# Normalized rows laid over the turned ones, other engine orders in the route stage, repacks by ScalarE, stores of stacked rows awaited one stage later

## The reference, cut to what matters

```python
xn = _layernorm(x)                       # 8 x 512 rows of 256
# attention branch, 16 heads of 16
q, k, v = heads(xn @ Wq + bq), heads(xn @ Wk + bk), heads(xn @ Wv + bv)
scores = (q k^T + q . dist_emb[l - r] + k . dist_emb[l - r]) / 4
s = layer_norm(softmax(scores) v @ Wo + bo + xn) * ln_gamma + ln_beta
# expert branch
n = layer_norm(xn, g1, be1); x1 = xn + n + (n @ mix_w + mix_b)
z = layer_norm(x1, g2, be2)
probs = softmax(z @ router_w)            # 8 experts, the best 2 kept
y = sum over the 2 of prob * (silu(z @ w1[e] + b1[e]) @ w2[e] + b2[e])
out = x + s * silu(x1 + y)
```

## Time and profile before

| | us |
|---|---|
| median of 3 runs | 2009.68 (2009.1 to 2012.36) |
| profiled execution | 2002.44, of which 2000.9 from first to last instruction |
| busy: TensorE, VectorE, ScalarE, GpSimd | 1626.6, 1235.0, 1129.1, 560.9 |
| route stage | 126 to 345 |
| experts stage | 349 to 1294 |
| mean granted TensorE clock | 0.909 of full speed |

### The profile page before, as it was taken

One profiled execution on the slowest core, in us unless ns is written; L12 is line 12 of the kernel. 1 busy time (PEld: TensorE's weight loads), 2 busy tenths in 40 slices (PEclk: granted clock), 3 DMA queues, 4 the chain that ended last, 5 costly groups with the idle time before them and its releaser, 6 DMA issues. The chain is left out here.

```text
span 2000.9 us, 32700 instructions
## 1 busy us (share of the span) xinstructions
PE 1626.6 (81%) x11256; PEld 1180.2 (59%) x11256; DVE 1235.0 (62%) x3009; ACT 1129.1 (56%) x1994; POOL 560.9 (28%) x662
## 2 busy tenths in 40 slices
PE   5758620787999899989999899759999999999981
PEld 3325320676788778877887788635555555555540
DVE  6755561621565546454646465758988888888860
ACT  2433310125656374736564556259888888888960
POOL 1352446320000000101000000014253654555454
PEclk9887655898999899999999999969999999999995
DMA  6463445996887897999887877689989989999931
GB/s 208 169 210 108 137 134 178 234 277 201 302 295 251 276 331 258 327 333 377 298 307 247 278 247 269 243 275 316 330 266 324 295 281 333 293 288 329 313 115 42
DMA packets 227381, 514.96 MB, mean 257 GB/s; under 512 B 37328, under 2 KB 83920, under 8 KB 222736
## 3 DMA queue, kind: packets, MB, share of 16 engines
q1 hardware_dynamic: 201856, 410.03, 63.6%
q0 software_dynamic: 24208, 98.65, 14.8%
q10 hardware_dynamic: 1152, 4.19, 0.5%
HBM read 367.08 MB, written 199.23 MB: 283 GB/s over the span
## 5 line engine op out<-in xcount | busy, mean ns | idle before, releaser
L983 DVE TENSOR_TENSOR rel_out<-rl,rel_tile 128x1024 f32<-128x1024 f32 x256 | 400.4, 1569 | 358.2 <-PE rl L1036 326.8
L960 ACT COPY rel_tile<-rl 128x1024 f32<-128x1024 f32 x256 | 377.0, 1476 | 297.7 <-DVE rel_out L983 164.7
L1273 ACT ACTIVATE scores<-scores,row_least 128x512 f32<-128x512 f32 x512 | 366.0, 718 | 35.5 <-DVE row_least L1309 33.2
L1309 DVE CUSTOM_DVE_ANT_1 scores<-sc,rq 128x512 f32<-128x512 f32 x512 | 338.6, 686 | 68.5 <-issue 57.7
L1413 PE MATMUL pt<-ident,scores 128*128 128x128 f32 x2048 | 321.9, 281 | 32.8 <-ACT probsT L1280 25.3
L1057 PE MATMUL up<-rowsT,w_b 128*128 128x256 f32 x1280 | 317.5, 394 | 4.4 <-DVE rowsT L989 2.3
L1413 PEld LDWEIGHTS pt<-ident,scores 128*128 128x128 f32 x2048 | 249.0, 145 | 115.7 <-DVE probsT L1317 35.9
L1070 PE MATMUL dn<-w_b,hid 128*128 128x256 f32 x1280 | 307.8, 385 | 0.0
L1057 PEld LDWEIGHTS up<-rowsT,w_b 128*128 128x128 f32 x1280 | 237.9, 195 | 33.8 <-DVE rowsT L989 5.0
L1070 PEld LDWEIGHTS dn<-w_b,hid 128*128 128x128 f32 x1280 | 233.1, 191 | 25.9
L1405 PE MATMUL sc<-ks,qs 96*128 96x512 bf16 x512 | 204.2, 399 | 32.9 <-DMA ks<-scratch_parts 20.0
(11 more groups left out here) (188 smaller groups left out, 1670.5 us busy)
## 6 DMA issues: line engine op xcount, KB each, us to landing
scratch_rel<-rel_out SPq DMA_DIRECT2D x256, 512.0 KB, 3.8
rq<-scratch_rel SPq DMA_DIRECT2D x256, 512.0 KB
krows_sb<-scratch_stack SPq DMA_DIRECT2D x768, 64.0 KB, 3.1
w_b<-in_w POOLq DMA_DIRECT2D x40, 1152.0 KB
w_b<-in_w POOLq DMA_DIRECT2D x40, 1028.0 KB
scratch_parts<-part SPq DMA_DIRECT2D x96, 128.0 KB
qrows_sb<-scratch_stack SPq DMA_DIRECT2D x192, 64.0 KB, 3.3
qs<-scratch_parts SPq DMA_DIRECT2D x192, 64.0 KB
```

What stands on the lines that cost most here:

```text
L960: nc.scalar.copy(square(tile)[:, :, u * UN:(u + 1) * UN], rl[r][:].rearrange("p a (b l) -> p l (a b)", l=TILE)).then_inc(s_kc, 1)
L983: nc.vector.tensor_tensor(out[n % SRING][:], rl[r][:].rearrange("p a (b s) -> p (a b) s", s=TILE), square(tile)[:, u * UN:(u + 1) * UN], A ...
L1273: nc.scalar.activation(sm[j][:, i], sm[j][:, i], ACT.Exp, bias=least[:, j, i:i + 1], scale=-1.0, accum_out=es[:, g // 2 % 2, i, 2 * j + g ...
L1309: nc.vector.tensor_tensor_reduce(sm[j][:, i].rearrange("p (c s) -> p c s", c=LT), sc[i % 2][:].rearrange("p (c s) -> p c s", c=LT), rq[j][ ...
```

## The change

- `z` is no longer a pair of buffers. The z of pair p lies over `xnT` of batches 2p and 2p + 1, so there are four, and the wait on the scatters (L598) is gone.
- GpSimd shifts all eight batches first and then stores x1 of batches 0 to 3.
- ScalarE, VectorE and TensorE have new orders. ScalarE repacks batches 0 to 5, the last three of them after all else; VectorE repacks 6 and 7 after `finish`.
- The wait for the two stores of `by_row` moves from the end of route to the experts stage: SyncE waits before its first loads from `stack`, and VectorE before its first late repack. `by_row`, `rel_tile` and the `part` buffers of the project stage take one place, which nothing else uses until the experts stage ends.

```diff
-        z = [sb(f"z{i}", [P, PAIR, E]) for i in range(ZRING)]
+        z = [xnT[:, 2 * p:2 * p + 2].rearrange("p b k s -> p (b k s)").rearrange("p (i e) -> p i e", e=E) for p in range(B // 2)]
...
         def repack_done(eng, b):
-            eng.wait_ge((s_ba, s_bd)[b % 2], b // 2 + 1)
+            eng.wait_ge(*((s_ba, b + 1) if b < ACT_REPACKS else (s_bd, b - ACT_REPACKS + 1)))
...
-                sp.dma_start(dst, by_row[:, i * TILE:(i + 1) * TILE]).then_inc(s_bs, 16)
-            sp.wait_ge(s_bs, 16 * 2)
+                sp.dma_start(dst, by_row[:, i * TILE:(i + 1) * TILE]).then_inc(keep["first_half"], 16)
...
             for b in range(B):
                 shifted(b)
-                if 1 < b < 6:
-                    store_x1(b - 2)
+            for b in range(4):
+                store_x1(b)
...
-                after(dve, s_sc, 16 * TOPK * PAIR * (p - ZRING + 1))
```

In the experts stage:

```diff
             for b in range(B):
                 after(sp, s_br, b - 1)
                 ...
+            sp.wait_ge(first_half, 16 * 2)
             for x in range(KRING):
                 load_k(x)
...
             def repack(b):
+                if b == 0:
+                    dve.wait_ge(first_half, 16 * 2)
                 dve.wait_ge(s_bh[b % 2], 16 * (b // 2 + 1))
```

More of the change, by code:

```diff
@@ L540, in repack @@
                 nc.scalar.copy(*repacked(b)).then_inc(s_ba, 1)
[L542 to L546, removed]
+            for b in range(4):
+                take_v(b)
             take_turned(0)
             take_turned(1)
-            repack(2)
[L550 to L561, removed]
+            exponents(0)
+            take_v(4)
+            take_turned(2)
+            take_v(5)
+            take_turned(3)
+            repack(0)
+            take_v(6)
+            take_turned(4)
+            exponents(1)
+            take_turned(5)
+            repack(1)
+            take_v(7)
+            repack(2)
             exponents(2)
@@ L565, in _ @@
             exponents(3)
+            for b in range(3, ACT_REPACKS):
+                repack(b)
             for i in range(2):
@@ L701, in _ @@
             residual(1)
+            residual(2)
             normalized(0)
-            residual(2)
             residual(3)
             normalized(1)
-            repack(1)
             shift(0)
@@ L728, in _ @@
             finish()
+            for b in range(ACT_REPACKS, B):
+                repack(b)
         @block.tensor
@@ L819, in experts @@
         by_head = [sb(f"late_by_head{i}", [KS, H, 2 * TILE], BF16) for i in range(2)]
-        with nc.sbuf_tensor("late_by_row", [KS, 2 * TILE, BH], BF16) as by_row:
-            pass
-        both = sb("rel_tile", [P, TILE, TILE])
+        by_row, both, first_half = keep["by_row"], keep["rel_tile"], keep["first_half"]
         out = [sb(f"rel_out{i}", [P, UN, TILE]) for i in range(SRING)]
@@ L1492, in program @@
         }
[L1493 to L1501, removed]
+        with nc.sbuf_tensor("by_row", [KS, 2 * TILE, BH], BF16) as by_row:
+            pass
+        with ExitStack() as one_place:
+            part = [[one_place.enter_context(nc.sbuf_tensor(f"part{i}_{k}", [P, 4, S], BF16)) for k in range(PARTS)] for i in range(PRING)]
+        with nc.sbuf_tensor("rel_tile", [P, TILE, TILE], F32) as square, nc.semaphore("first_half_stored") as first_half:
+            halves = dict(keep, part=part, by_row=by_row, rel_tile=square, first_half=first_half)
+            with nc.sbuf_tensor("xn_all", [P, NT, E], F32) as xn, nc.sbuf_tensor("xnT_all", [P, B, KC, S], F32) as xnT, \
+                    nc.sbuf_tensor("wv_mix", [P, KC, 2 * E], F32) as wvm, nc.sbuf_tensor("rms2", [P, NT], F32) as rms2, \
+                    nc.sbuf_tensor("tri_sb", [P, P], F32) as tri, nc.sbuf_tensor("router_sb", [P, KC, NE], F32) as rw, \
+                    nc.sbuf_tensor("first_row", [P, NE], F32) as first_row, nc.sbuf_tensor("turn_no", [P, NBLK], F32) as turn_no, \
+                    nc.sbuf_tensor("cvec", [P, E], F32) as cvec:
+                early = dict(halves, xn=xn, xnT=xnT, wvm=wvm, rms2=rms2, tri=tri, rw=rw, first_row=first_row, turn_no=turn_no, cvec=cvec)
+                project(nc, t, early)
+                route(nc, t, early)
+            experts(nc, t, halves)
         attention(nc, t, keep)
```

23 lines of the change are left out of this document (10 added, 13 removed).

## The result

The changed kernel takes 1998.88 us (median of 20 runs), the kernel before 2009.97 us in the same jobs: a ratio of 0.9943 (95% interval 0.9931 to 0.9956), 11.1 us faster where 22.2 were forecast, and just above the forecast's range of 1972 to 1998.

A forecast was written before the change was run, and what follows sets the result against it. The prediction took the route stage's loop of GpSimd scatters and VectorE's z as the bound: 27.9 us gained at pair 2, less 5.7 for held scatters, gives 22.2, so 2009.68 becomes 1987.5 us, range 1972 to 1998.

The forecast's parts named there:

- The loop: Route stage: z waits for scatters, scatters for VectorE's slots; the loop takes 24 us of each 44.8 us period.
- Starts of pairs 0, 1, 2: Route stage: scatters start at 186.3, 221.9 and 256.4 us, pair 2 being 27.9 us earlier.
- Repacks 6 and 7 hold the scatters: Route stage: two VectorE copies of 4.7 us hold GpSimd for 9.4 us instead of 3.7, 5.7 us lost.
- The tail: End of route: 19.7 us from first blank row to the experts stage's first load stay, so earlier scatters move everything after.
- the moved wait: Route to experts stage: stores of by_row land by 315, first late repack is at 338.8; spare 24 us, cost 0.
- (c): Rival: gain comes back in the experts stage, whose first weights come late beside the by_row store unfinished at 326; chance 0.04.
- (d): Rival: first late repack waits for the by_row stores, slower if they land after 361, 2019 us at 370; chance 0.03.
- Experts stage of equal length: Experts stage: keeps its length, its first stall of 17.23 us of ScalarE moving with the stage start.
- my own sign: Experts stage: the prediction is wrong if this stage is longer than before by over 4 us.
- Copies and z beside scatters: Route stage: VectorE copies hold GpSimd's scatters to their end, 9.4 us; z beside GpSimd's work costs 2 us.
- Rival (b): Route stage: z of pair 3 gets locked by scatters of pair 1, losing 4 to 9 us, say 1994 us; chance 0.18.

The follow-up runs named there:

- changed_again: The changed kernel itself, unaltered, run once more in the third job: ratio 0.9906 to the kernel before.
- changed_third: The changed kernel itself, unaltered, run once more in the fourth job: ratio 0.9946 to the kernel before.
- before_itself: The kernel before, unaltered, profiled again in the fourth job: ratio 1.0.
- store_after_scatters: The changed kernel, but SyncE issues the two stores of stacked rows only when all GpSimd rows have landed: ratio 0.9986 to the kernel before.
- orders_only: The changed kernel with z back in two buffers and its wait on scatters of two pairs before: ratio 0.9969 to the kernel before.
- four_by_head: The changed kernel with four buffers instead of two for the loads of the repack: ratio 0.9933 to the kernel before.
- the third job: Three runs against the kernel before: changed kernel again 0.9906, kernel before with only z over xnT 0.992, changed kernel with repacks as early as possible 0.9792.
- the fourth job: Three repeats against the kernel before: changed kernel 0.9946, kernel before 1.0, changed kernel with repacks moved into idle gaps 0.9893.

## Why the prediction was wrong

- **The loop.** Right. The waits of z on scatters are gone, and the edit of z alone moves the stage start by 14 us (the medians by 18, in both jobs).
- **Starts of pairs 0, 1, 2.** Right within 0.5, 3.4 and 1.3 us, the last two partly by luck: the trace has a pause of 7.7 us that I didn't have, and without it the starts are 218.0 and 250.3, 4 and 6 us earlier than I said. I had set TensorE's pace too low: v_and_mix(5) and (6) take 8.81 us each in changed_again, where I had 10.1, as in its row for (6):

```profile
195.50 8.81 PE L733 MATMUL v_mix<-wv_mix,xnT_all 128*128 128x512 f32 x16
```

- **Repacks 6 and 7 hold the scatters.** Right in the issue: 5.05 and 5.36 us against 0.97, 8.5 us in all against 9.4 forecast. Wrong in the sum: it was not on the path that ended the stage, as all repacks by ScalarE show.
- **The tail, the step that failed.** The 19.7 us "of blank rows, landing and stage change" were carried over as a constant, so that an earlier start "moves all that follows by as much", and the stores, which "land by 315", were put at "cost 0". They landed in time for those who wait for them (q1 is empty soon after 316, and in changed_again and changed_third the later store lands 32.5 and 32.4 us after its issue, where I had 29.4): the moved wait costs nothing. But they filled the DMA engines in front of another queue's rows. The tail took 30.0 us, 10.3 more than forecast; of the 22.2, 11.9 were left, and 11.55 is what the stage start shows. I asked who waits for the stores, and not who shares the engines with them. In the kernel before, 51 us of GpSimd's issues lay behind the stores and hid them.
- **(c) and (d).** (c) had the right engines but the wrong side of the stage change: it asked for stores unfinished at 326, and they had already cost 10 us before the stage began. It came true only when the stores were issued at 316. (d) came true in no run: the longest wait for a late repack was for its load.
- **Experts stage of equal length.** From SyncE's first load to TensorE's first scores of attention it took 963.9 us before (965.5 in before_itself), 969.8, 972.6 and 968.8 in the three traces of the changed kernel, and 965.2 to 976.0 in the others (997.6 in store_after_scatters), with the new memory layout and without. So some 3 to 9 us may be given back there, and by my own sign (longer by over 4 us) this part of the prediction failed in the profiled pair: the changed kernel starts its stage 11.55 us earlier and attention only 5.6. The kernels that start the stage latest (before, before_itself, orders_only, at 346 to 351) have 963.9 to 965.5 us, but four_by_head has 965.2 from 338.6. No row names a cause, and the medians (11.1) agree with the 11.55 at the start; it stays open.
- **Copies and z beside scatters.** The Trainium skill ("SBUF — State Buffer", section "Who interferes with whom") has copies of VectorE that lock out GpSimd's descriptor writing: the trace agrees on the hold, 5.05 and 5.36 us; in which mode the copies ran, no trace shows. Rival (b) did not happen: z of pair 3 took 2.75 us for eight beside the scatters of pair 1, against 2.67 in the earlier trace rows.

```profile
239.73 2.75 DVE L597 TENSOR_SCALAR xnT_all<-xn_all,mv,work 128x256 f32<-128x256 f32 x8
```

## What to carry to other kernels

When a change brings forward the last issue of a stage, its tail is not a constant: add up the bytes in flight from there on in all queues, and divide by what the DMA engines move in that stretch. Here that would have been 10.6 MB; at the 252 GB/s that were measured they take the 42 us found, at the 300 GB/s of the row from 314 to 318 only 35. A bulk store that nobody waits for soon still delays every queue beside it, and what is issued behind it in its own, so issue it when the engines are half idle: with the stores out of the tail the ratio was 0.9883 against 0.9943, while the new orders alone gave 0.9969. And before a change of orders, try the removal of the false dependence alone, here an edit of two lines: in the job that had both, it gave as much as the whole change, as far as runs tell (0.992 and 0.9906).

## What the runs showed of the hardware that I had not expected

**Small writes of one queue beside large ones of another.** The rows above: GpSimd's queue got 5.0% of the engines while q1 had 82.5%, and moved most of its bytes when the stores were nearly done (1.56 MB in 308 to 316, 1.91 MB from there on). Issued behind the same stores, a load of 768 KB in SyncE's own queue took 40.6 us instead of 5.5 to 12.4.

**A pause behind TensorE's signals.** The first rows show ScalarE between repack 0 and take_v(6) in the changed kernel, the second the same place in changed_again:

```profile
193.70 7.22 ACT L539 COPY by_row<-by_head 96x4096 bf16<-96x4096 bf16 x1
208.59 1.20 ACT L521 COPY va<-v_mix 128x256 f32<-128x256 f32 x4 [7.67 <-remote]
```
```profile
193.54 7.24 ACT L539 COPY by_row<-by_head 96x4096 bf16<-96x4096 bf16 x1
200.68 0.63 ACT L521 COPY va<-v_mix 128x256 f32<-128x256 f32 x2
```

The same program has 7.67 us of idle time there in one execution, and none in another. The profile names no releaser ("remote"), but the semaphore increments in the trace tell what ScalarE waited for: TensorE's count for each of the four banks. In changed_again these counts are recorded 0.02 us after the ends of the matmuls (198.32 to 204.33). In the changed kernel the matmuls' rows end at 197.63 to 202.78, and the counts are recorded at 208.56 to 208.74. VectorE has shorter idle times of the kind, 1.8 and 2.5 us; the first, up to 205.73, ends with TensorE's count for logits(3), recorded at 205.70, when the matmuls' rows end at 195.81. So these engines stand for TensorE. Whether its matmuls or only its signals were late can't be told, since the ends of matmuls are modelled.

The pause was there in ten profiles of eight kernels with the new orders, all of which record the count for logits(3) 5.3 to 9.9 us late, and in neither of the two of the third job; the kernel before and the one with z alone don't show it in any job. What holds TensorE back stays open: the load beside it is excluded (four_by_head), and so is the chip alone, since the third and the fourth job ran on the same one. It goes with the program and with the job. In the changed kernel it is worth 8 to 9 us at the stage start (337.4 and 338.6 against 329.2), and 0.4% of the ratio (0.9943 and 0.9946 against 0.9906).
